# Heads interleaved over the partitions of queries and keys, with five of 32 mask additions moved from TensorE to DVE

## What is computed

```python
q, k, v = (proj(Wq, bq), proj(Wk, bk), proj(Wv, bv))          # 8 heads of 32
scores = jnp.einsum('bhqd,bhkd->bhqk', q, k) / np.sqrt(D_HEAD)
mask = adj + jnp.eye(n, dtype=adj.dtype)[None] > 0
scores = jnp.where(mask[:, None], scores, -jnp.inf)
attn = jax.nn.softmax(scores, axis=-1)
out = jnp.einsum('bhqk,bhkd->bhqd', attn, v)
h = x + out @ Wo.T + bo                                        # heads put side by side again
x = (h - mu) * jax.lax.rsqrt(var + EPS) * gamma + beta         # layer 0 ends

feat_proj = jnp.einsum('bnh,oh->bno', x, fc_w) + fc_b          # layer 1
logits = q + jnp.swapaxes(k, 2, 1)                             # one number per node each
masked = logits + (1.0 - adj_mat) * NEG_INF                    # then leaky relu, softmax
out = jnp.einsum('bnm,bmh->bnh', atten, feat_proj) + x
```

## Time and profile before

| | us |
|---|---|
| median of 3 runs | 1147.71 (1142.61 to 1153.31) |
| the profiled execution's own time | 1145.0 |
| its span, first to last instruction | 1143.2 |
| PE busy | 1039.5 (91%) |
| DVE busy | 737.4 (65%) |
| POOL busy | 723.1 (63%) |
| ACT busy | 624.2 (55%) |
| mean granted clock of TensorE | 0.964 of full speed |

### The profile page before, as it was taken

The page is one execution under the profiler, slowest core; times in us unless marked ns, Lnnn a source line. Parts: engine busy times, 40 slices in busy tenths (PEclk is TensorE's granted clock), DMA queues, the critical chain, the costliest instruction groups (busy, mean ns, idle before and its releaser), DMA issues. The chain is left out here.

```text
span 1143.2 us, 17238 instructions
## 1 busy us (share of the span) xinstructions
PE 1039.5 (91%) x5800; PEld 656.8 (57%) x5800; DVE 737.4 (65%) x1863; ACT 624.2 (55%) x1178; POOL 723.1 (63%) x415
## 2 busy tenths in 40 slices
PE   4789898989989899998999999999989999899856
PEld 4444465646656565665656566565656656565545
DVE  4555775766757677576767767676777757575432
ACT  2145465565646657455565656466565646556543
POOL 3056786665767676577776657677666667668751
PEclk9789999999989999999999999999999999899989
DMA  4335434443433544343354534334453434333010
GB/s 134 93 103 151 116 96 123 111 122 83 126 96 93 139 103 116 99 127 107 91 146 111 136 75 126 103 99 135 107 139 93 116 102 120 101 90 103 28 46 28
DMA packets 90759, 120.97 MB, mean 106 GB/s; under 512 B 18480, under 2 KB 45616, under 8 KB 90672
## 3 DMA queue, kind: packets, MB, share of 16 engines
q1 hardware_dynamic: 90672, 119.87, 39.4%
HBM read 52.44 MB, written 8.39 MB: 53 GB/s over the span
## 5 line engine op out<-in xcount | busy, mean ns | idle before, releaser
L694 ACT ACTIVATE e<-st_bank 128x512 f32<-128x512 f32 x512 | 307.7, 602 | 438.5 <-PE st_bank L521 432.6
L900 DVE CUSTOM_DVE_ANT_0 sm_bank<-sm_bank,masks 128x512 f32<-128x512 f32 x512 | 355.0, 695 | 269.9 <-PE sm_bank L529 265.6
L529 PE MATMUL sm_bank<-kt_hi,q_pad 128*128 128x512 f32 x512 | 299.5, 587 | 57.1 <-issue 47.9
L981 POOL TENSOR_TENSOR e_sum<-e_sum,e 128x1024 f32<-128x1024 f32 x128 | 303.3, 2388 | 53.3 <-ACT e L694 53.2
L519 PE MATMUL st_bank<-q_stack,k_stack 97*128 97x512 f32 x512 | 238.8, 467 | 2.2 <-ACT e L694 1.8
L521 PE MATMUL st_bank<-mask_t,ident_b 128*128 128x512 bf16 x512 | 202.3, 395 | 0.0
L981 POOL TENSOR_TENSOR e_sum<-e 128x1024 f32<-128x1024 f32 x64 | 152.2, 2379 | 76.4 <-ACT e L694 67.8
L519 PEld LDWEIGHTS st_bank<-q_stack,k_stack 97*128 97x128 f32 x512 | 97.6, 191 | 138.6 <-ACT e L694 127.5
L529 PEld LDWEIGHTS sm_bank<-kt_hi,q_pad 128*128 128x128 f32 x512 | 105.4, 206 | 66.8 <-issue 58.4
L504 PE MATMUL shared<-feat,z 128*128 128x256 f32 x512 | 137.9, 419 | 2.1 <-ACT z L640 2.1
L461 PE MATMUL o_bank<-e,v 128*32 128x512 f32 x1024 | 137.2, 608 | 0.7 <-ACT e L694 0.7
(11 more groups left out here) (126 smaller groups left out, 1725.4 us busy)
## 6 DMA issues: line engine op xcount, KB each, us to landing
adj_in<-in_adj SPq DMA_DIRECT2D x32, 1024.0 KB, 5.7
q_stack<-qt_hi SPq DMA_DIRECT2D x256, 64.0 KB, 2.0
k_stack<-kt_hi SPq DMA_DIRECT2D x256, 64.0 KB, 2.0
x_in<-in_x SPq DMA_DIRECT2D x16, 512.0 KB, 4.1
q_pad<-qt_hi SPq DMA_DIRECT2D x128, 64.0 KB, 2.0
q_stack<-qt_lo SPq DMA_DIRECT2D x128, 64.0 KB, 2.0
k_stack<-kt_lo SPq DMA_DIRECT2D x128, 64.0 KB, 2.0
h<-in_x SPq DMA_DIRECT2D x16, 512.0 KB, 3.9
```

The source lines that it names most:

```text
L529: nc.tensor.matmul(sm_bank[s % 2][:, :], q_pad[j // GH][:, j % GH, qt * P:(qt + 1) * P], kt_hi[j // GH][:, :], start=True, stop=True).then ...
L694: nc.scalar.activation(e[:, kt, i, :], st_bank[s % 2][:, :], ACT.Exp, scale=SCALE)\
L900: nc.vector.tensor_tensor_reduce(sm_bank[s % 2][:, :], sm_bank[s % 2][:, :], mask[nxt if off else par][:, qt * N:(qt + 1) * N], 1.0, LOWES ...
L981: nc.gpsimd.tensor_tensor(e_sum[:, pair, :], a, b, ALU.add).then_inc(pool_done.sem, 1)
```

## The change

Queries and keys are laid out so that partition `4 d + i` holds dimension `d` of head `i`, where it was `32 i + d`. For this the columns of `Wq` and `Wk` are permuted once, when the weights are copied in the set-up (two instructions of 256 columns in place of one of 512, on ACT and on DVE, for each of the two matrices), and the biases are loaded in the same order (four DMAs of one column in place of two). In this layout the source of a stack, read partition by partition, is already ordered as 32 dimensions by 4 heads, so one DMA of 256 KB fills one part for all four heads: `stack` issues 6 DMAs where it issued 24. `pad` still issues four of 64 KB; each reads and writes every fourth partition.

At steps 12, 14, 15, 26 and 29 PE no longer multiplies the mask into the bank. DVE adds `mask_t` to the bank in place, ahead of its maximum of that step, and ACT's exponential waits for DVE's signal instead of PE's.

```diff
...
+DVE_MASKED = (12, 14, 15, 26, 29)
...
+        st_masked = Signal(sem("st_masked"), [(s, 0) for s in DVE_MASKED])
...
@@ -256,8 +258,9 @@
                 sp.dma_start(col, b.rearrange("(g p) -> p g", p=P),
                              allow_slow_non_contiguous=True).then_inc(cols_loaded, 16)
             for k, b in enumerate((bq, bk)):
-                sp.dma_start(bias_col[:, k, :], b.rearrange("(g p) -> p g", p=P),
-                             allow_slow_non_contiguous=True).then_inc(const_loaded, 16)
+                for g in range(NG):
+                    sp.dma_start(bias_col[:, k, g:g + 1], b[g * P:(g + 1) * P].rearrange("(i d) -> d i", i=GH),
+                                 allow_slow_non_contiguous=True).then_inc(const_loaded, 16)
             sp.dma_start(adj_in[:, :, :], rows(adj, 0)).then_inc(adj_loaded.sem, 16)
             for row, b in ((gamma_row, gamma), (rest_row, beta), (bo_row, bo), (fcb_row, fc_b)):
                 sp.dma_start(row[:, :], b.partition_broadcast(P)).then_inc(const_loaded, 16)
@@ -269,19 +272,17 @@
             def stack(g, t):
 
                 sp.wait_ge(dve_done.sem, dve_done.after(f"k_lo{g}", t if g == 0 else t - 1))
-                for i in range(GH):
-                    r = slice(DH * i, DH * (i + 1))
-                    for part, (q_part, k_part) in enumerate(((qt_hi, kt_hi), (qt_lo, kt_hi), (qt_hi, kt_lo))):
-                        to = slice(DH * part, DH * (part + 1))
-                        sp.dma_start(f(q_stack[g][to, i, :]), f(q_part[g][r, :])).then_inc(stacked[g].sem, 16)
-                        sp.dma_start(f(k_stack[g][to, i, :]), f(k_part[g][r, :])).then_inc(stacked[g].sem, 16)
+                for part, (q_part, k_part) in enumerate(((qt_hi, kt_hi), (qt_lo, kt_hi), (qt_hi, kt_lo))):
+                    to = slice(DH * part, DH * (part + 1))
+                    sp.dma_start(f(q_stack[g][to, :, :]), f(q_part[g][:, :])).then_inc(stacked[g].sem, 16)
+                    sp.dma_start(f(k_stack[g][to, :, :]), f(k_part[g][:, :])).then_inc(stacked[g].sem, 16)
 
             def pad(g, t):
 
                 sp.wait_ge(act_done.sem, act_done.after(f"q_hi{g}", t))
                 sp.wait_ge(sm_done.sem, sm_done.after((GH * NT - 1 - LEAD) % POS if g == 0 else (POS - 1 - LEAD) % POS, t - 1 if g == 0 else t))
                 for i in range(GH):
-                    r = slice(DH * i, DH * (i + 1))
+                    r = slice(i, P, GH)
                     sp.dma_start(f(q_pad[g][r, i, :]), f(qt_hi[g][r, :])).then_inc(padded[g].sem, 16)
 
             def place_max(g, t):
@@ -516,10 +517,14 @@
                                 pe.wait_ge(act_done.sem, act_done.after("mt1", t - 1))
                         pe.wait_ge(exp_done.sem, exp_done.after((s - 2) % POS, t if s >= 2 else t - 1))
                         bank = st_bank[s % 2]
-                        nc.tensor.matmul(bank[:, :], k_stack[g][:, i, kt * P:(kt + 1) * P], q_stack[g][:, i, :],
-                                         start=True, stop=False)
-                        nc.tensor.matmul(bank[:, :], ident_b[:, :], mask_t[par][:, kt, :],
-                                         start=False, stop=True).then_inc(st_done.sem, 1)
+                        if s in DVE_MASKED:
+                            nc.tensor.matmul(bank[:, :], k_stack[g][:, i, kt * P:(kt + 1) * P], q_stack[g][:, i, :],
+                                             start=True, stop=True).then_inc(st_done.sem, 1)
+                        else:
+                            nc.tensor.matmul(bank[:, :], k_stack[g][:, i, kt * P:(kt + 1) * P], q_stack[g][:, i, :],
+                                             start=True, stop=False)
+                            nc.tensor.matmul(bank[:, :], ident_b[:, :], mask_t[par][:, kt, :],
+                                             start=False, stop=True).then_inc(st_done.sem, 1)
                     off, j, qt = maxima_tile(s)
                     if on(t, off):
                         if j % GH == 0 and qt == 0:
@@ -604,7 +609,13 @@
             banks = [*shared, *sm_bank]
             for k in range(4):
                 act.wait_ge(setup_pe, k + 1)
-                nc.scalar.copy(weight_hi[:, k, :, :], banks[k][:, :].rearrange("p (i o) -> p i o", i=DT)).then_inc(setup_act, 1)
+                if k in (WQ, WK):
+                    for i in range(DT):
+                        last = nc.scalar.copy(weight_hi[:, k, i, :].rearrange("p (g d h) -> p g d h", g=NG, h=GH),
+                                              banks[k][:, i * D:(i + 1) * D].rearrange("p (g h d) -> p g d h", g=NG, h=GH))
+                else:
+                    last = nc.scalar.copy(weight_hi[:, k, :, :], banks[k][:, :].rearrange("p (i o) -> p i o", i=DT))
+                last.then_inc(setup_act, 1)
             act.wait_ge(setup_pe, 5)
             nc.scalar.copy(scratch[:, 6, :], banks[4][:, :]).then_inc(setup_act, 1)
             act.wait_ge(cols_loaded, 16 * N_COLS)
@@ -679,7 +690,10 @@
                 for s in range(POS):
                     g, kt, i = s // (POS // 2), s // GH % NT, s % GH
                     if on(t, 0):
-                        act.wait_ge(st_done.sem, st_done.after(s, t))
+                        if s in DVE_MASKED:
+                            act.wait_ge(st_masked.sem, st_masked.after(s, t))
+                        else:
+                            act.wait_ge(st_done.sem, st_done.after(s, t))
                         if i == 0:
                             n = max(kt, 1)
                             if g == 1:
@@ -777,8 +791,16 @@
             banks = [*shared, *sm_bank]
             for k in range(4):
                 dve.wait_ge(setup_act, k + 1)
-                nc.vector.tensor_tensor(weight_lo[:, k, :, :], banks[k][:, :].rearrange("p (i o) -> p i o", i=DT),
-                                        f(weight_hi[:, k, :, :]), ALU.subtract).then_inc(setup_dve, 1)
+                if k in (WQ, WK):
+                    for i in range(DT):
+                        last = nc.vector.tensor_tensor(weight_lo[:, k, i, :].rearrange("p (g d h) -> p g d h", g=NG, h=GH),
+                                                       banks[k][:, i * D:(i + 1) * D].rearrange("p (g h d) -> p g d h", g=NG, h=GH),
+                                                       f(weight_hi[:, k, i, :]).rearrange("p (g d h) -> p g d h", g=NG, h=GH),
+                                                       ALU.subtract)
+                else:
+                    last = nc.vector.tensor_tensor(weight_lo[:, k, :, :], banks[k][:, :].rearrange("p (i o) -> p i o", i=DT),
+                                                   f(weight_hi[:, k, :, :]), ALU.subtract)
+                last.then_inc(setup_dve, 1)
             dve.wait_ge(setup_act, 6)
             for i in range(DT):
                 last = nc.vector.scalar_tensor_tensor(weight_lo[:, FC, i, :], banks[4][:, i * D:(i + 1) * D], gamma_col[:, i:i + 1],
@@ -892,6 +914,12 @@
                         last.then_inc(done, 1)
 
                 for s in range(POS):
+                    if s in DVE_MASKED and on(t, 0):
+                        kt = s // GH % NT
+                        dve.wait_ge(act_done.sem, act_done.after("mt1", t - 1))
+                        dve.wait_ge(st_done.sem, st_done.after(s, t))
+                        nc.vector.tensor_tensor(st_bank[s % 2][:, :], st_bank[s % 2][:, :], mask_t[par][:, kt, :], ALU.add)\
+                            .then_inc(st_masked.sem, 1)
                     off, j, qt = maxima_tile(s)
                     if on(t, off):
                         if off == 1 and j == 0 and qt == 0:
```

More of the change, by code:

```diff
@@ L218, in build @@
         padded = [Signal(sem(f"padded{g}"), [(f"q{g}", 1)], 16 * GH) for g in range(NG)]
-        stacked = [Signal(sem("stacked0"), [("g0", 1)], 16 * 6 * GH), Signal(sem("stacked1"), [("g1", 0)], 16 * 6 * GH)]
+        stacked = [Signal(sem("stacked0"), [("g0", 1)], 16 * 6), Signal(sem("stacked1"), [("g1", 0)], 16 * 6)]
         max_placed = [Signal(sem(f"max_placed{g}"), [("max", 1 - g)], 16) for g in range(NG)]
@@ L223, in build @@
         weights_loaded, cols_loaded, const_loaded = sem("weights_loaded"), sem("cols_loaded"), sem("const_loaded")
-        N_WEIGHTS, N_COLS, N_CONST = 6, 3, 10
+        N_WEIGHTS, N_COLS, N_CONST = 6, 3, 12
         ident_made = sem("ident_made")
```

## The result

Changed kernel: median 1100.45 us of 4 runs (1094.32 to 1106.90). Kernel before, on the same chip: 1149.88 us of 4 runs (1142.61 to 1153.31). Ratio 0.958, 95% interval 0.950 to 0.966: 49 us faster, where 1059 us (86 to 91 us faster) was forecast. The result lies 12 us above the forecast range of 1042 to 1088. The profiled execution, the slowest of the four, took 1106.9 us with a span of 1104.8.

The account below looks back on a forecast made before the run. TensorE's (PE's) work was taken to set the time, with one hole at step 11. Sum: 1145.0 - 50.3 (waits) - 21.5 (clock) - 18.1 (masks) + 1.0 (set-up) + 3.0 (set back) = 1059.1 us; range 1042 to 1088.

Parts of the forecast that it names:

- the transfer of the big copies: Step 11: six stack copies drain at 227 GB/s, through by 516.7, so PE does not wait for the padded queries.
- the rival of slow copies: Big copies ahead of the padded queries in the DMA rings make the kernel slower below 98 GB/s; 1212 us at 80; chance 0.03.
- the hole: PE's idle time at step 11, before L529, waiting for the padded queries; removing such waits was to give 50.3 us.
- no change at step 11: Rival: something holds the padded queries as long as before, so only masks and set-up count; 1128 us, chance 0.04.
- SP's queue as the cause of the hole: 24 stack issues of 0.64 us each on SP delay the padded queries at step 11; six issues save 50.3 us.
- The clock as the second price of the hole: Behind step 11 the clock drops to 0.50 after PE stands still; without the hole 21.5 us are saved.
- 80 matmuls for 18.1 us: Five mask steps in 16 iterations leave PE, 0.233 us a matmul, 18.6 us less 0.5 for a POOL wait.
- DVE's additions cost nothing: 80 additions of 0.69 us, 55 us on DVE, stay covered; rival with half reaching PE: 1087 us, chance 0.05.
- Set-up, 1.0 us: Half copies of two weight matrices and two more DMA issues at the start add 1.0 us, between 0.3 and 4.
- The margin of `op0`: At step 15 `op0` waits for POOL with 0.6 us to spare; 0.2 us set back in 14 iterations, 3 us.
- Forecast for an iteration, 60.8 to 61.2 us: Sign of being right: an iteration takes 61.9 us less 1.2, plus what is set back.
- The range's lower end: 1042 us: nothing set back, clock -25, 2 us in the start, PE's short waits for ACT shrinking 0.4 us an iteration.

Follow-up runs that it names:

- rows spread: The spread kernel: changed kernel, but each part of a stack goes to every third of 96 partitions, not 32 adjacent ones; 1067.15 us, ratio 0.929.
- the four kernels in which the hole is gone: Spread rows with five masks on DVE (1067.15 us), none (1075.15) or seven (1064.17); changed kernel with four of group 1's stack copies issued behind the padded queries (1076.99).
- the layout alone: Changed kernel with all 32 masks back on PE, keeping the new layout and six copies a stack; 1103.7 us, ratio 0.9603.
- the small copies: Changed kernel with 24 copies of 64 KB a stack in place of six big ones, new layout and masks on DVE kept; 1141.58 us, ratio 0.994.
- the masks alone: Kernel before, with its old layout and 24 copies a stack, but the five mask additions on DVE; 1143.38 us, ratio 0.9951.

## Why the prediction was wrong, and where it was right

**The step that failed** is the transfer of the big copies: of the 102 GB/s I wrote "so this is no limit; 102 / 0.45 = 227 GB/s is, and gives 516.7. I take no wait." The big copies move 140 GB/s in the changed kernel and 127 by themselves. At 140, 1.57 MB take 11.2 us. Counted back from 498.5, where the rate rises, that begins at 487.3, about when the adjacency is through: the stretch from 486 to 488 still moved 338 GB/s. Only then does the transfer of the padded queries begin; issued from 492.4 on, they land about 8 us later. The edge of this was in the text twice: the 15.4 us that the 102 GB/s would give, set aside as "short of issues", and the rival of slow copies, which had the mechanism (the padded queries stand behind the six big copies) but which I counted only where the whole kernel becomes slower than before, below 98 GB/s, and gave 0.03. Between 98 and 227 GB/s lies a case that no rival covered: part of the hole stays. The rival "no change at step 11" (1128 us) and the forecast were its two ends. The Trainium skill ("SBUF — State Buffer", "Door 1: The DMA port swizzle") pointed the right way, that 32 adjacent partitions reach only 8 of 16 ports. The trace agrees on the direction. Its 189 GB/s is what the copies show from 32 partitions to 32 (188); from 128 partitions, as in this kernel, they show 127 to 140, and the waits at step 11 in the middle were up to 3.05 us where I had worked out up to 0.5 from the page.

What that step cost, in the twelve middle iterations. Forecast there: 36.7 us of holes (47.9 less the 3.2 at the start, 4.4 in the first two iterations and 3.6 in the tail), 17.2 of clock, 13.6 of masks, less 2.4 set back, together 65.1. Measured: 28.7. Of the holes 13.8 came instead of 36.7, of the clock 5.8 instead of 17.2, of the masks at most 9.1 instead of 13.6 (9.1 is all that PE's busy time lost at full clock). With the rows spread, the same stretch gave 797.97 - 732.43 = 65.5 us, so the mechanism and the sum stand once the transfer is what I had taken it for.

**Part by part.**
- *SP's queue as the cause of the hole*: right. With 24 issues in the new layout the hole is back (45.7 + 6.2 us); with six fast ones it is gone.
- *The clock as the second price of the hole*: right. It is 1.00 in all twelve iterations of each of the four kernels in which the hole is gone. Where it stays, the clock is below 1.00 in some of the twelve: one with the layout alone, six in the changed kernel, eight before, eleven with the small copies, twelve with the masks alone. In the twelve there is no drop without a hole, then, but not a drop behind every hole.
- *80 matmuls for 18.1 us*: mis-sized. 8.0 us where nothing else is in the way. I had priced all five at the 0.233 us of a step without other work. From one score matmul to the next, the spread kernel with masks on DVE saves against the layout alone 0.24 us at step 12, 0.22 at step 15 and 0.23 at step 26, but 0.05 at step 14 and 0.10 at step 29. Behind those two PE now waits in the next weight load, for ACT (layer 1 transposes) and for DVE (dot products). In one iteration of the spread kernel (steps 14 and 29):

```profile
490.81 0.42 PEld L495 LDWEIGHTS shared<-ident,z 128*128 128x128 f32 x4 [0.42 <-ACT split_hi L679]
...
521.38 0.19 PEld L387 LDWEIGHTS shared<-split_hi,uk_hi 128*128 128x128 f32 x1 [0.30 <-DVE q_dot L891]
```

  With the layout alone the first of these waits is 0.17 us, and the second does not occur.

- *DVE's additions cost nothing*: right in the middle. They take 0.701 us each (forecast 0.69). In the spread kernel PE's waits for the maxima and the exponentials are 4.4 and 3.5 us in all, and 7.0 of these 7.9 us lie in the start and the first two iterations. There they seem to cost a little: the first graph's iteration is 1.4 us longer with them (45.78 against 44.35).
- *Set-up, 1.0 us*: of the right size, as far as single executions tell. PE starts its first matmul with the padded queries at 30.58 in the changed kernel and at 30.28 to 30.65 in three others of the new layout; in the old one it is 29.98 before and 28.32 with the masks alone.
- *The margin of `op0`, set back as 3 us*: not needed in the middle. In the spread kernel PE waits before L387 for `split_lo` three times, 6.0 us in all, and never in the middle iterations.
- *Forecast for an iteration, 60.8 to 61.2 us*: met by the spread rows (60.95 to 61.38), in part because two errors cancel, the masks 0.4 too high and 0.2 set back for nothing.
- *The range's lower end*: its terms (3 us not set back, 3.5 more of clock, 2 in the start, 6.4 of short waits) add up to 1044, not 1042. The result lies on the other side, so nothing hangs on it.
- *The 8 us between 1059 and 1067* (10 in the profiled execution of 1068.98): they lie outside the twelve. I had 20.8 us of gain in the start, the first two iterations and the tail; the spread kernel shows 10.8 (76.3 us of span less 65.5). The first graph's iteration gained 6.7 us of the 8.9 that I had; the second became 2.3 us longer (62.61 against 60.35) where I had a gain. There PE waits 3.0 us for `split_lo`, against 2.6 before, and behind it the clock now drops, which it had not done before. I had priced drops behind step 11 alone.

The spread kernel in two stretches of that second iteration, the first with the wait in it; the clock is the third number from the end:

```profile
115.00:130.00 15.00, 10.85 (x51) 6.50 (x51) 10.79 (x25) 5.06 (x9) 14.84 (x9) 0.89 0.56 145
130.00:145.00 15.00, 14.95 (x85) 8.72 (x86) 9.99 (x27) 8.88 (x16) 5.96 (x6) 0.88 0.44 120
```

Before, the clock was 1.00 throughout this iteration.

**What stays open.** Why a source of 128 partitions makes the copy into a slow target slower than one of 32 does (127 against 188 GB/s). Why moving the masks alone brings a clock drop into all twelve iterations. And why the hole with the big copies varies from one iteration to the next, between 0 and 3 us, while the copies are the same. Their rate does not settle it: in the changed kernel it was 144 GB/s (617 to 619) ahead of a hole of 0.95 us, 131 (679 to 681) ahead of one of 3.05 us, but 152 (808 to 810) ahead of one of 2.74 us. No run here tells more.

## What to carry to other kernels

Fewer and bigger DMAs free the queue that issues them, but whatever is issued next stands behind them in the rings: look where the waiting copy is then, and how fast what is ahead drains. A busy share below 1 is no headroom for another shape; between a measured rate and an extrapolated one the forecast needs a case for what lies between. A copy that fills 32 partitions is better spread with a stride over more of them (235 and 380 GB/s here, against 127), where the order of the rows is free, as it is in a contraction. And a matmul taken away is worth its duration only at steps at which PE waits for nobody.

## What the runs showed of the hardware that I had not expected

- The target's placement changes the rate of the same bytes by a factor of three: 127 GB/s into 32 adjacent partitions, 235 into every third of 96, 380 into every fourth of 128.
- The source counts as well: 188 GB/s from 32 partitions to 32 adjacent ones, 127 from 128.
- A wait of 3.0 us of PE had a clock drop behind it at the second graph of the spread kernel, where one of 2.6 us in the kernel before had none. Holes of 1 to 3 us at step 11 had one in some iterations only, and not by their length: in the changed kernel the one of 3.05 us had none, and one of 1.63 us had. A hole costs its length, and where the drop comes some 2 us more: 1.9 in the changed kernel (11.45 us in six iterations), 2.15 before.
